# Layer norms as two block instructions, small router and decay sums in PSUM banks, and a low half formed by VectorE

## What is computed

```python
x = x + attn_a(_layernorm(x))   # linear attention with a decay per channel, its own norm, Wo
x = x + ffn(_layernorm(x))      # 8 experts, every token through all of them
x = x + attn_b(_layernorm(x))   # recurrence on an 8x8 state per head, 16 heads, then norm, gate and MLP
x = x + ffn(_layernorm(x))      # the same weights again
```

```python
router_probs = softmax(x @ w_router); gate_weights = softmax(x @ w_gating / 0.1)
h = silu(x @ w_gate[e]) * (x @ w_up[e]);  expert_out[e] = h @ w_down[e]
cw = router_probs * gate_weights
cw = cw / (sum(cw, -1, keepdims=True) + 1e-09)
out = sum_e expert_out[e] * cw[e]
```

## Time and profile before

| what | value |
|---|---|
| median of 3 runs | 961.81 us |
| the profiled execution, and its span | 961.01 us, 959.3 us |
| PE busy | 864.3 us (90%) |
| PE weight load busy | 728.3 us (76%) |
| DVE busy | 589.2 us (61%) |
| ACT busy | 401.9 us (42%) |
| POOL busy | 411.2 us (43%) |
| mean granted TensorE clock | 0.954 |

### The profile page before, as it was taken

How to read it: one execution, slowest core, us unless ns; L and a number is a source line. 1 busy time by engine, 2 the same in 40 slices (tenths; PEclk the granted TensorE clock), 3 DMA queues, 4 the chain that set the end, 5 groups by cost and what they waited for, 6 DMA issues and landing times.

```text
span 959.3 us, 13871 instructions
## 1 busy us (share of the span) xinstructions
PE 864.3 (90%) x5170; PEld 728.3 (76%) x5170; DVE 589.2 (61%) x979; ACT 401.9 (42%) x878; POOL 411.2 (43%) x296
## 2 busy tenths in 40 slices
PE   4399999989898899999987969798999789999997
PEld 1387987778767779997665658687998668788886
DVE  6559644388918993239589896988113968532322
ACT  5143347633264233335655346123333244453333
POOL 3434311056703876536244543567653534211111
PEclk9599999999899999999997789999999989999999
DMA  9300000011001100022111001111002211000000
GB/s 283 84 1 1 1 1 1 1 44 44 23 23 44 45 23 23 1 88 89 44 44 45 22 23 45 45 44 44 12 1 88 89 52 48 1 1 12 1 1 12
DMA packets 20711, 35.88 MB, mean 37 GB/s; under 512 B 3062, under 2 KB 9636, under 8 KB 20644
## 3 DMA queue, kind: packets, MB, share of 16 engines
q1 hardware_dynamic: 20644, 35.00, 11.1%
HBM read 21.36 MB, written 13.63 MB: 36 GB/s over the span
## 4 chain that ended last, share of the span: by engine, by line
PE 54%; DVE 17%; issue 4%; ACT 2%; POOL 1%; DVEq 0%; ACTq 0%; POOLq 0%
PE bank L1219 53%; DVE sh_buf L1661 1%; DVE normed L1548 1%; DVE states L1873 1%; DVE state L1777 1%; DVE low L1675 1%; DVE w_a L1875 1%; DVE state L1788 1%; DVE scr L1881 1%; DVE backs L1856 1%; DVE work L1752 1%; DVE work L1771 1%; PE bank L1233 0%; ACT sh_buf L1048 0%; DVE quad L1743 0%
## 5 line engine op out<-in xcount | busy, mean ns | idle before, releaser
L1661 DVE TENSOR_TENSOR sh_buf<-sh_buf,bank 128x512 f32<-128x512 f32 x256 | 172.6, 683 | 276.7 <-PE bank L1219 229.4
L1219 PEld LDWEIGHTS bank<-w_down,sh_buf 128*128 128x128 f32 x2048 | 283.9, 197 | 74.5 <-DVE sh_buf L1661 47.1
L1219 PE MATMUL bank<-w_down,sh_buf 128*128 128x128 f32 x2048 | 304.2, 285 | 38.0 <-DVE sh_buf L1661 37.9
L1048 ACT ACTIVATE sh_buf<-bank 128x512 f32<-128x512 f32 x256 | 152.8, 598 | 305.9 <-PE bank L1219 233.7
L1219 PE MATMUL bank<-z_lo,w_hi 128*128 128x512 f32 x512 | 238.9, 467 | 0.0
L1219 PE MATMUL bank<-z_hi,w_hi 128*128 128x512 f32 x512 | 205.5, 401 | 0.0
L1219 PE MATMUL bank<-z_hi,w_lo 128*128 128x512 f32 x512 | 205.0, 400 | 0.0
L945 POOL TENSOR_TENSOR x<-x,y_weighted 128x512 f32<-128x512 f32 x64 | 85.2, 1331 | 248.6 <-ACT y_weighted L1162 248.6
L1219 PEld LDWEIGHTS bank<-z_hi,w_hi 128*128 128x128 f32 x512 | 98.3, 192 | 24.1
L1219 PEld LDWEIGHTS bank<-z_lo,w_hi 128*128 128x128 f32 x512 | 100.0, 195 | 10.8 <-issue 4.1
L1219 PEld LDWEIGHTS bank<-z_hi,w_lo 128*128 128x128 f32 x512 | 100.0, 195 | 7.8 <-issue 0.7
(11 more groups left out here) (207 smaller groups left out, 992.9 us busy)
## 6 DMA issues: line engine op xcount, KB each, us to landing
trans_spill<-state SPq DMA_DIRECT2D x16, 512.0 KB, 2.6
backs<-trans_spill SPq DMA_DIRECT2D x16, 512.0 KB, 3.3
backs<-keep_spill SPq DMA_DIRECT2D x4, 1024.0 KB, 5.5
x<-in_x SPq DMA_DIRECT2D x4, 256.0 KB, 5.7
backs<-in_w_gate SPq DMA_DIRECT2D x4, 256.0 KB, 5.7
backs<-in_w_up SPq DMA_DIRECT2D x4, 256.0 KB, 5.9
keep_spill<-rkv SPq DMA_DIRECT2D x4, 256.0 KB, 2.5
keep_spill<-low SPq DMA_DIRECT2D x4, 256.0 KB, 2.6
```

The costliest lines, as they stand in the source:

```text
L1048: act.activation(s_buf[:, m % 2, :], bank_of("gate", m)[:], ACT.Silu).then_inc(S["silu_done"], 1)
L1219: return pe.matmul(dst, lhs, rhs, start=start, stop=stop, **kw)
L1661: dve.tensor_tensor(h_buf[:, m % 4, :], s_buf[:, m % 2, :], bank_of("up", m)[:], ALU.mult).then_inc(S["h_done"], 1)
```

## The change

- `ln_normalise` becomes two instructions over all four tiles: `ln_centre` (tiles minus mean, 128x512) and `ln_scale` (times the inverse root, 128x512). Only the second waits for POOL, and the planner may put other work between the two. For `mid` the centring itself frees the bank, and the two `tick` instructions go.
- `z_lo` is bank minus `z_hi`, by VectorE (`z_low`, L1673 in the new program). ScalarE makes `z_hi` first; `zf` is copied after the subtraction (`ffn_copy`), and only the router waits for it. The transposes' bank is held until `zf` is copied, and POOL's subtraction is gone.
- The router's shifted logits, the first softmax's exponentials and the small sums lie in the router's bank, which is held until the weights are done (`cw_rdy`) and no longer only until `logits`. The two divisions are merged: w = ab / (sum(ab) + 1e-9 sum(a) sum(b)), eight instructions for nine, none of them with two inputs in SBUF.
- The sums of logarithms lie in a bank (`lend_log` takes it, the exponentials free it). The first sum reads `log_end` in SBUF, the other three a tile in the bank.
- The last expert's output of the last pass is scaled and added by VectorE (`add_last`), four instructions that read the bank.
- `WEIGHT` of ScalarE goes from 1.20 to 1.10 and all of `LEAD` is replaced, so that the order changes in most places. The first value of `PE_SUMS` is changed too; it belongs to a step that isn't summed and does nothing.

The diff's core, without the planner's numbers, the semaphores' names and the calls:

```diff
@@ -67,12 +67,12 @@
-WEIGHT = dict(pe=1.60, act=1.20, dve=1.31, pool=1.10, sp=1.02)
+WEIGHT = dict(pe=1.60, act=1.10, dve=1.31, pool=1.10, sp=1.02)
@@ -164,12 +165,13 @@
-def norm(kind, n, after, z_act, z_after=(), stats=1.72, norm=1.37, port=False):
+def norm(kind, n, after, z_act, z_after=(), stats=1.72, norm=0.7, port=False, centre=True, freer=None):
...
-            dve((k + "norm", n), norm, on("pool", k + "stats", n)),
-            pe((k + "z", n), 0.66, on("dve", k + "norm", n), *z_after, takes=(((k + "z", n), on("act", k + "z", n)),)),
+            dve((k + "centre", n), 0.7, on("dve", k + "stats", n), port=centre),
+            dve((k + "norm", n), norm, on("pool", k + "stats", n), on("dve", k + "centre", n), port=True),
+            pe((k + "z", n), 0.66, on("dve", k + "norm", n), *z_after, takes=(((k + "z", n), freer or on("act", k + "z", n)),)),
@@ -718,6 +720,12 @@
         def on_pe(part, t):
...
+        def logs(j):
+            return bank_of("log", j)[:].rearrange("p (g c) -> p g c", g=G)
+        def route_part(q, first, n, e=1):
+            return bank_of("route", q)[:, first:first + n * e].rearrange("p (n e) -> p n e", e=e)
@@ -869,13 +877,6 @@
-            def z_low(q):
-                pool.wait_ge(S["ln_out"], LN["ffn", q] + 1)
-                if q >= 2:
-                    pool.wait_ge(S["u_full"], CHUNKS * (q - 1))
-                pool.tensor_tensor(z_lo[:, q % 2, :], zf[:], z_hi[:, q % 2, :].bitcast(F32), ALU.subtract).then_inc(S["z_low"], 1)
@@ -1025,20 +1024,22 @@
             def ffn_z(q):
...
-                src = bank_of("ffn_z", q)
+                if q >= 2:
+                    act.wait_ge(S["u_full"], CHUNKS * (q - 1))
+                act.activation(z_hi[:, q % 2, :], bank_of("ffn_z", q)[:], ACT.Copy).then_inc(S["ln_out"], 1)
+            def ffn_copy(q):
+                act.wait_ge(S["z_low"], q + 1)
...
-                    act.wait_ge(S["z_low"], q)
-                step.inc(act.activation(zf[:], src[:], ACT.Copy))
-                if q >= 2:
-                    act.wait_ge(S["u_full"], CHUNKS * (q - 1))
-                act.activation(z_hi[:, q % 2, :], src[:], ACT.Copy).then_inc(S["ln_out"], 1)
+                act.activation(zf[:], bank_of("ffn_z", q)[:], ACT.Copy).then_inc(S["zf_rdy"], 1)
             def ffn_exp(q):
...
-                pr = probs[:].rearrange("p (g s) e -> p g s e", s=2)
-                act.activation(pr[:, :, 0, :], pr[:, :, 0, :], ACT.Exp).then_inc(S["probs_rdy"], 1)
-                act.activation(pr[:, :, 1, :], pr[:, :, 1, :], ACT.Exp, scale=10.0).then_inc(S["probs_rdy"], 1)
+                pr = route_part(q, 64, 2 * G, E).rearrange("p (g s) e -> p g s e", s=2)
+                act.activation(route_part(q, 128, G, E), pr[:, :, 0, :], ACT.Exp).then_inc(S["probs_rdy"], 1)
+                act.activation(chances_b[:], pr[:, :, 1, :], ACT.Exp, scale=10.0).then_inc(S["probs_rdy"], 1)
@@ -1103,8 +1104,8 @@
-                act.activation(cumdec[:, 1:G + 1, :], td, ACT.Exp, scale=-DECAY / 2).then_inc(S["ew_exp"], 1)
-                act.activation(invdec, td, ACT.Exp, scale=DECAY / 2).then_inc(S["ew_exp"], 1)
+                act.activation(cumdec[:, 1:G + 1, :], logs(j), ACT.Exp, scale=-DECAY / 2).then_inc(S["ew_exp"], 1)
+                act.activation(invdec, logs(j), ACT.Exp, scale=DECAY / 2).then_inc(S["ew_exp"], 1)
@@ -1232,7 +1235,7 @@
-                free[name] = (S["ln_out"], n + 1)
+                free[name] = (S["zf_rdy"], j + 1) if kind == "ffn" else (S["ln_out"], n + 1)
@@ -1292,13 +1295,13 @@
             def router(q):
...
-                pe.wait_ge(S["ln_out"], LN["ffn", q] + 1)
+                pe.wait_ge(S["zf_rdy"], q + 1)
...
-                free[name] = (S["rl_used"], q + 1)
+                free[name] = (S["cw_rdy"], q + 1)
@@ -1542,15 +1553,16 @@
-            def ln_normalise(n, tiles, last_sem="ln_norm"):
+            def per_tile(v):
+                return v.unsqueeze(2).broadcast_to((P, G, C))
+            def ln_centre(n, tiles):
+                return dve.tensor_tensor(normed[:, n % 2], tiles, per_tile(mean_var[:, n % 2, :, 0]), ALU.subtract)
+            def ln_scale(n):
...
-                for i in range(G):
-                    ins = dve.tensor_scalar(normed[:, n % 2, i, :], tiles[:, i, :], mean_var[:, n % 2, i, 0:1],
-                                            rstd[:, n % 2, i:i + 1], ALU.subtract, ALU.mult)
-                    if i < G - 1 or not last_sem:
-                        step.inc(ins)
-                if last_sem:
-                    ins.then_inc(S[last_sem], 1)
+                step.wait()
+                return dve.tensor_tensor(normed[:, n % 2], normed[:, n % 2], per_tile(rstd[:, n % 2, :]), ALU.mult)
@@ -1600,13 +1612,6 @@
             def inner(q):
...
-            def mid_norm(q):
-                ln_normalise(LN["mid", q], inner(q), None)
-                step.wait()
-                dve.tensor_scalar(tick[:, 0:1], neg_half[:], 1.0, None, ALU.mult).then_inc(S["inner_read"], 1)
-                dve.tensor_scalar(tick[:, 1:2], neg_half[:], 1.0, None, ALU.mult).then_inc(S["ln_norm"], 1)
@@ -1626,24 +1631,20 @@
-                pr = probs[:].rearrange("p (g s) e -> p g s e", s=2)
-                step.inc(dve.tensor_reduce(psum_[:], probs[:], AX_X, ALU.add))
-                step.inc(dve.tensor_tensor(w, pr[:, :, 0, :], pr[:, :, 1, :], ALU.mult))
-                step.wait()
-                step.inc(dve.reciprocal(prec[:], psum_[:]))
-                step.wait()
-                pc = prec[:].rearrange("p (g s) -> p g s", s=2)
-                step.inc(dve.tensor_tensor(pscale[:], pc[:, :, 0], pc[:, :, 1], ALU.mult))
-                step.wait()
-                step.inc(dve.tensor_tensor(w, w, pscale[:].unsqueeze(2).broadcast_to((P, G, E)), ALU.mult))
-                step.wait()
-                step.inc(dve.tensor_reduce(cwsum[:], w, AX_X, ALU.add))
-                step.wait()
-                step.inc(dve.tensor_scalar(cwsum[:], cwsum[:], 1e-9, None, ALU.add))
-                step.wait()
-                step.inc(dve.reciprocal(pscale[:], cwsum[:]))
-                step.wait()
-                dve.tensor_tensor(w, w, pscale[:].unsqueeze(2).broadcast_to((P, G, E)), ALU.mult).then_inc(S["cw_rdy"], 1)
+                chances_a, sums_a, total, inverse = route_part(q, 128, G, E), route_part(q, 192, G), route_part(q, 196, G), route_part(q, 200, G)
+                step.inc(dve.tensor_reduce(sums_a, chances_a, AX_X, ALU.add))
+                step.inc(dve.tensor_reduce(sums_b[:], chances_b[:], AX_X, ALU.add))
+                step.inc(dve.tensor_tensor(w, chances_a, chances_b[:], ALU.mult))
+                step.wait()
+                step.inc(dve.tensor_tensor(both[:], sums_a.rearrange("p n e -> p (n e)"), sums_b[:], ALU.mult))
+                step.inc(dve.tensor_reduce(total, w, AX_X, ALU.add))
+                step.wait()
+                step.inc(dve.scalar_tensor_tensor(out=total, in0=both[:].unsqueeze(2), scalar=1e-9, in1=total, op0=ALU.mult, op1=ALU.add))
+                step.wait()
+                step.inc(dve.reciprocal(inverse, total))
+                step.wait()
+                dve.tensor_tensor(w, w, inverse.broadcast_to((P, G, E)), ALU.mult).then_inc(S["cw_rdy"], 1)
@@ -1666,16 +1667,24 @@
             def spread(v):
...
+            def z_low(q):
+                dve.wait_ge(S["ln_out"], LN["ffn", q] + 1)
+                dve.tensor_tensor(z_lo[:, q % 2, :], bank_of("ffn_z", q)[:], z_hi[:, q % 2, :].bitcast(F32),
+                                  ALU.subtract).then_inc(S["z_low"], 1)
             def front_log(j):
...
+                if lent_log[j]:
+                    dve.wait_ge(*lent_log[j])
...
-                    step.inc(dve.scalar_tensor_tensor(out=td[:, i, :], in0=td[:, i, :], scalar=1.0,
-                                                      in1=td[:, i - 1, :] if i else log_end[:], op0=ALU.add, op1=ALU.add))
-                step.wait()
-                dve.tensor_copy(log_end[:], td[:, G - 1, :]).then_inc(S["ew_log"], 1)
+                    step.inc(dve.scalar_tensor_tensor(out=logs(j)[:, i, :], in0=td[:, i, :], scalar=1.0,
+                                                      in1=logs(j)[:, i - 1, :] if i else log_end[:], op0=ALU.add, op1=ALU.add))
+                step.wait()
+                dve.tensor_copy(log_end[:], logs(j)[:, G - 1, :]).then_inc(S["ew_log"], 1)
@@ -1906,14 +1915,33 @@
+            def add_last():
+                q, e = PASSES - 1, E - 1
+                dve.wait_ge(S["y_full"], PASSES * E)
+                dve.wait_ge(S["x_added"], PASSES * E - 1)
+                dve.wait_ge(S["cw_rdy"], PASSES)
+                for i in range(G):
+                    ins = dve.scalar_tensor_tensor(out=xt(BLOCKS - 1)[:, i, :], in0=bank_of("y", PASSES * E - 1)[:, i * P:(i + 1) * P],
+                                                   scalar=cw[:, q % 2, i, e:e + 1], in1=xt(BLOCKS - 1)[:, i, :], op0=ALU.mult, op1=ALU.add)
+                    if i < G - 1:
```

(3 more changed lines are left out.)

85 lines of the change are left out of this document (52 added, 33 removed).

## The result

The changed kernel takes 926.6 us, the median of four runs (925.21 to 928.58); on the same chip the kernel before took 961.96 (960.07 to 962.64). The ratio is 0.9637, with a 95% interval of 0.9613 to 0.9661: 35 us faster, where 10 were forecast (952 from 961.8). The profiled execution took 925.21 us and has a span of 923.2.

A forecast was written before the change was run, and what follows sets the result against it. PE is full from 48 to 192 and 360 to 432 us; in stretches with gaps VectorE, held by POOL, was taken as the limit. Terms -2.0 - 1.15 - 5.6 = -8.8 from 961.0 gave 952 us, range 940 to 963.

The forecast's parts named there:

- The start: Chain to PE's first chunk in pass 0: first chunk at 45.4 us instead of 48.03, -2.0 with the `in` norms' +0.6.
- The +0.6 of the `in` norms: At the start, the first `in` norm as blocks ends later, at 10.2 us instead of 9.49; +0.6 counted.
- The end: Last expert's scaling and adding: 2.55 us by ScalarE and POOL becomes four VectorE instructions priced 1.36, -1.15.
- The meetings go: Stretches with gaps: VectorE no longer held by POOL in weights, logarithms, norms, -16.8; added work +5.6; net -11.2 us of VectorE.
- -6.0 and +3.0: Norms: half of 11.9 us of being held by POOL goes, -6.0; ten norms as two longer blocks add +3.0.
- I take half: -5.6: Stretches with gaps: half of VectorE's net -11.2 us reaches the end; bounds were none and all of it.
- The planner's new numbers count for nothing in it: Whole kernel: the new `WEIGHT` and `LEAD` were given no share in the forecast of 952 us.
- Rival A: All -11.2 arrives, norms freed entirely (-6.0 more), gaps between 672 and 840 us filled, say 4: 941 us; chance 0.18.
- The clock: Argument for rival A: clock is below 1.00 in stretches with gaps, so fewer gaps may quicken PE; no size given.
- Rival B: The middle gives nothing, meetings with POOL only move: 958 us, or 961 with half the added work; chance 0.18.
- Rival C: Banks run short because weights and logarithms hold them, so PE's chunks wait: +14, 966 us; chance 0.14.
- below 48: A: Sign for rival A: PE's idle time from 192 to 840 us falls from 59.3 to below 48; forecast about 54.

## Why the prediction was wrong

- **The start: right.** -2.0 was forecast for the first chunk and it is 45.57 - 48.03 = -2.46, with each link of the chain within 0.2 us of its forecast. The +0.6 of the `in` norms did not come. The last tenths are luck: in the other kernels with the new forms there this chunk starts between 44.7 and 46.5 us.
- **The end: right.** -1.15 was forecast, and 2.55 to 1.13 is -1.4.
- **The meetings go: right in kind, short in size, and this step failed.** The sum has -11.2 us of VectorE. With the old numbers VectorE's busy time fell by 17.6 (589.2 to 571.6), with the new ones by 27.2. The weights fell as priced, from 19.1 to 11.4 us (with one instruction fewer; -6.7 forecast, -7.7), and so did the four sums of logarithms, from 11.4 to 6.5 (-5.1 forecast, -4.9). The norms were mis-sized: -6.0 and +3.0 had been put down, -3, and they fell from 46.7 to 34.7, -12.0, and with the old numbers to 38.8, -7.9. Two things were short in it. The 11.9 us counted three norms, while the trace before has four more of 1.9 to 2.2 us, and one of 4.60 us at 406 us, where PE is full; all together are held 19.1 us. And the half that I took is near what blocks at the old place show (6.9 of 11.9 us); the new list moved them out of POOL's way.
- **"I take half: -5.6": not what made the sum short, and not a fixed share.** With the old numbers the time fell by 13.9 us; less 2.0 at the start and 1.4 at the end it is 10.5 for 17.6 us of VectorE, 0.6 of it. With all of the -11.2 instead of half the sum of the prediction would have been 961.8 - 14.4 = 947.4, and that kernel takes 947.31; this agreement is a match of sums, of a share too large with an amount too small. Single holds were passed on whole at one place (7.4 and 3.8 us) and not at all at another (2.1 us), and 14.2 us less of VectorE gave nothing with the old operations and the new numbers. VectorE's 83% over 240 us could not tell these apart: where single holds pass on whole, in the new kernel from the 129th to the 137th product, it is busy 32.6 of 39.2 us, 83% as well.
- **"The planner's new numbers count for nothing in it": failed, and this is the larger miss.** They are worth 20.7 us with the new operations; the list that comes out of them is about 15 us better even with the old forms. This term had no price, no bounds and so no part in the range. Rival A came nearest, with gaps filled between 672 and 840 us, "say 4": PE's idle time there fell from 11.0 to 5.8 us, but the larger fill, 18.4 us, was between 192 and 672.
- **The clock.** A said that fewer gaps may quicken PE, and put nothing down for it. 14.1 of the 36.1 us of span came in PE's busy time.
- Rival B fell: PE's idle time from 192 to 840 us went from 59.3 to 36.1 us and not to 59 or more. Rival C fell for this list: PE never waits for the bank that the weights free. Its mechanism is real, though: without leads PE waits 7.5 us for it. The prediction's mark "below 48: A" came true.

The Trainium skill (SBUF — State Buffer, "The single rule: only the shared port pair causes contention") was right about the blocks: at the old place they are held once each, 2.60 and 2.66 us. The Trainium skill's longer fixed part for an instruction that reads a bank (VectorE: DVE Perf Modes, "The TRN2 errata — SBUF-src ops pay a fixed extra latency per instruction") would have added 2.3 us by the prediction's estimate. The small instructions of the weights show at most a fifth of it: the last product takes 0.186 us with the bank and 0.192 without, the reciprocal of the sum 0.191 and 0.178. The copy behind the logarithm sums does show it, 0.29 us from the bank (534.73 us) for 0.23 from SBUF, as the norm on a tile did.
